# Cross-attention with a dense mixture of experts on one core: four slots of expert activations, one of down weights, and down rows spread over every expert step

## The reference

```python
q = layernorm(x) @ Wq + bq;  k = ctx @ Wk + bk;  v = ctx @ Wv + bv
x = x + softmax(q @ k.T / sqrt(256)) @ v          # for each of 16 sequences
h = layernorm(x)
router = softmax(h @ w_router); gate = softmax((h @ w_gating) / 0.1)
for e in range(8):                                # F = 1024
    expert[e] = (silu(h @ w_gate[e]) * (h @ w_up[e])) @ w_down[e]
cw = router * gate;  cw = cw / (sum(cw) + 1e-9)
out = x + sum_e expert[e] * cw[:, e]              # every expert sees every token
```

## Time and profile before

| | |
|---|---|
| profiled execution | 1101.56 us, of which the span of the core is 1099.8 us |
| PE busy | 1021.7 us (93%), 6160 matmuls |
| DVE busy | 789.0 us (72%) |
| POOL busy | 643.7 us (59%) |
| ACT busy | 499.1 us (45%) |
| mean granted TensorE clock | 0.969 of full |
| DMA | 40.61 MB, mean 37 GB/s |

### The profile page before, as it was taken

The page is one execution under the profiler, slowest core; times in us unless marked ns, Lnnn a source line. Parts: engine busy times, 40 slices in busy tenths (PEclk is TensorE's granted clock), DMA queues, the critical chain, the costliest instruction groups (busy, mean ns, idle before and its releaser), DMA issues.

```text
span 1099.8 us, 16297 instructions
## 1 busy us (share of the span) xinstructions
PE 1021.7 (93%) x6160; PEld 941.5 (86%) x6160; DVE 789.0 (72%) x1361; ACT 499.1 (45%) x874; POOL 643.7 (59%) x532
## 2 busy tenths in 40 slices
PE   6877787999999999999999999999999999999998
PEld 5877776988888888888888889988888888888888
DVE  4876737777777777777777777777777777777775
ACT  3676545444444443444444434444444444444432
POOL 3456526666656566666665656565666666565632
PEclk7898887999999999999999999999999999999999
DMA  6121104000101010101010101010100101010001
GB/s 164 69 91 54 37 12 150 26 33 21 39 20 40 20 39 20 40 11 40 8 40 20 39 20 39 20 39 20 38 21 20 39 21 39 20 39 1 1 1 67
DMA packets 37462, 40.61 MB, mean 37 GB/s; under 512 B 2760, under 2 KB 35384, under 8 KB 37384
## 3 DMA queue, kind: packets, MB, share of 16 engines
q1 hardware_dynamic: 37384, 39.58, 11.5%
HBM read 35.90 MB, written 3.67 MB: 36 GB/s over the span
## 4 chain that ended last, share of the span: by engine, by line
PE 53%; DVE 24%; POOL 10%; issue 4%; ACT 4%; DMA 4%; DVEq 0%; SPq 0%; POOLq 0%; ACTq 0%
PE ps L248 51%; POOL arena L411 7%; DVE xsacc L867 3%; DMA shared<-in_ctx 3%; DVE shared L856 2%; DVE shared L811 2%; DVE shared L833 2%; DVE shared L827 2%; DVE shared L813 2%; DVE shared L819 2%; ACT arena L594 2%; DVE shared L831 2%; DVE shared L846 2%; DVE shared L851 2%; DVE shared L837 1%
## 5 line engine op out<-in xcount | busy, mean ns | idle before, releaser
L411 POOL TENSOR_TENSOR arena<-shared,arena 128x448 fp32r<-128x448 f32 x256 | 311.7, 1233 | 309.1 <-ACT arena L594 306.2
L248 PE MATMUL ps<-arena 128*128 128x256 f32 (+4 forms) x3120 | 425.3, 289 | 7.8 <-DVE arena L252 5.5
L248 PEld LDWEIGHTS ps<-arena 128*128 128x128 f32 (+2 forms) x3120 | 414.4, 194 | 15.0 <-DVE arena L252 4.5
L248 PE MATMUL ps<-xc_hi,w_hi 128*128 128x448 f32 x896 | 342.0, 382 | 38.0 <-DVE shared L807 17.1
L248 PE MATMUL ps<-xc_lo,w_hi 128*128 128x448 f32 x896 | 329.8, 368 | 0.0
L248 PE MATMUL ps<-xc_hi,w_lo 128*128 128x448 f32 x896 | 329.8, 368 | 0.0
L248 PEld LDWEIGHTS ps<-xc_hi,w_hi 128*128 128x128 f32 x896 | 170.9, 191 | 80.3 <-DVE shared L807 28.2
L587 ACT ACTIVATE shared<-shared 128x448 f32<-128x448 f32 x192 | 109.6, 580 | 203.3 <-DVE shared L817 119.1
L248 PEld LDWEIGHTS ps<-xc_hi,w_lo 128*128 128x128 f32 x896 | 170.3, 190 | 14.4
L248 PEld LDWEIGHTS ps<-xc_lo,w_hi 128*128 128x128 f32 x896 | 171.2, 191 | 9.0
L594 ACT CAST arena<-shared 128x448 fp32r<-128x448 f32 x256 | 141.1, 567 | 75.6 <-DVE shared L851 55.4
(11 more groups left out here) (123 smaller groups left out, 930.0 us busy)
## 6 DMA issues: line engine op xcount, KB each, us to landing
early<-in_L_ffn_w_down SPq DMA_DIRECT2D x16, 512.0 KB, 3.9
shared<-in_ctx SPq DMA_DIRECT2D x8, 750.0 KB
w_raw<-in_L_ffn_w_gate SPq DMA_DIRECT2D x17, 256.0 KB, 2.8
w_raw<-in_L_ffn_w_up SPq DMA_DIRECT2D x17, 256.0 KB, 3.1
early<-in_L_ffn_w_gate SPq DMA_DIRECT2D x15, 256.0 KB, 2.7
early<-in_L_ffn_w_up SPq DMA_DIRECT2D x15, 256.0 KB, 3.1
x_dram<-xsacc SPq DMA_DIRECT2D x8, 224.0 KB, 5.6
xsacc<-x_dram SPq DMA_DIRECT2D x1, 1792.0 KB, 10.7
```

The costliest lines, as they stand in the source:

```text
L248: ins = nc.tensor.matmul(dst, w, m, start=first and i == 0, stop=last and i == len(passes) - 1, skip_group_check=onto)
L411: nc.gpsimd.tensor_tensor(h[:, 1, j, at:at + TC], tile, h[:, 0, j, at:at + TC].bitcast(fp32), ALU.subtract).then_inc(hid_lo_done, 1)
```

## The change

1. **Slots.** `HSLOTS` is 4, `wd` has one slot. ACT rounds the down weights of a half only when PE has finished all row tiles of the half before (`row_ready`), now in the third quad of the half itself, and POOL's low part follows. SP issues the load of the next down weights behind the two weight sets.
2. **Down rows.** In PE's list the row tiles of group g are 0 and 1 at the end of the even quad, 2, 3 and 4 in the odd quad, 5 and 6 in the next even quad; DVE's `add_rows` move accordingly.
3. **Temporaries.** `u21` and `u12` have two tiles each, by the parity of the quad; `up_u2` and ACT's `up_first` wait for the low parts of quad n-2.
4. **Combine weights** are computed on DVE at the ends of quads 1 and 2 and awaited in quad 3.
5. **Attention.** Contexts are loaded by halves (one sequence each) with a semaphore for each, and earlier at the start. `norm_terms` on POOL has two operations instead of four; DVE makes the other two (`tensor_scalar`). `maxima` and the exponentials are done for each sequence apart. POOL's preparing work is moved behind later parts (`low_set(0)` behind `add_bv(4)`, `low_set(1)` to the end of pair 7), `high_comb` and `high_set(1)` on ACT and the sums of `xf` on DVE to other pairs.

In the fence are the parts that the prediction speaks of; renamings are left out.

```diff
-    HSLOTS = 3
+    HSLOTS = 4
...
+        u21 = [up_t[:, 0, :], sb("u21_odd", [P, TC])[:, :]]
+        u12 = [up_t[:, 1, :], xsacc[:, TILES * D:TILES * D + TC]]
         g21, g12, g22, g11 = [gate_t[:, i, :] for i in range(4)]
-        u21, u12, u22 = [up_t[:, i, :] for i in range(3)]
+        u22 = up_t[:, 2, :]
...
-        HS, WD = 2 * 2 * TH, 2 * FT * D
-        hs = [arena[:, a:a + HS].rearrange("p (l j t) -> p l j t", l=2, j=2) for a in (0, 2 * HS + WD, HS)]
-        wd = [arena[:, a:a + WD].rearrange("p (l t d) -> p l t d", l=2, t=FT) for a in (3 * HS + WD, 2 * HS)]
+        hs = [arena[:, a:a + HS].rearrange("p (l j t) -> p l j t", l=2, j=2) for a in (0, 2 * HS + WD, HS, 3 * HS + WD)]
+        wd = arena[:, 2 * HS:2 * HS + WD].rearrange("p (l t d) -> p l t d", l=2, t=FT)
...
+            def load_ctx_half(p, b):
+                sp.dma_start(ctx_raw[:, p % 2, b], ctx_v[p][:, b]).then_inc(ctx_in[p % 2][b], DMA)
+            load_ctx_half(0, 0)
...
-            sp.dma_start(ctx_raw[:, 0], ctx_v[0]).then_inc(ctx_in, DMA)
+            load_ctx_half(0, 1)
             sp.dma_start(xs[:, 2:4, :], x_v[:, 2:4, :]).then_inc(x_parts[1], DMA)
+            for b in range(2):
+                load_ctx_half(1, b)
+            sp.dma_start(wv_raw, wv.rearrange("(k p) n -> p k n", p=P)).then_inc(wv_in, DMA)
...
             def load_ctx(p):
-                sp.wait_ge(ctx_in, DMA * p)
-                at_least(sp, ct_ready, 2 * (p - 1))
-                at_least(sp, cn_lo_done, 2 * (p - 1))
-                sp.dma_start(ctx_raw[:, p % 2], ctx_v[p]).then_inc(ctx_in, DMA)
+                for b in range(2):
+                    sp.wait_ge(ct_ready, 2 * (p - 2) + b + 1)
+                    sp.wait_ge(cn_lo_done, 2 * (p - 2) + b + 1)
+                    load_ctx_half(p, b)
...
             for hn in range(1, SETS):
                 if hn + 1 < SETS:
-                    load_down(hn + 1)
                     load_set(2 * hn + 2)
                     load_set(2 * hn + 3)
+                    load_down(hn + 1)
...
-            def norm_terms(mv, var, root, shift, bias, n, steps, done):
-                nc.gpsimd.tensor_tensor(var, mv[:, :, 1], eps_c[:, 0:n], ALU.add).then_inc(norm_step, 1)
-                pool.wait_ge(norm_step, steps + 1)
+            def norm_terms(var, root, shift, bias, n, step, done):
                 nc.gpsimd.tensor_tensor(root, var, power_c[:, 0:n], ALU.pow).then_inc(norm_step, 1)
-                pool.wait_ge(norm_step, steps + 2)
-                nc.gpsimd.tensor_tensor(shift, mv[:, :, 0], root, ALU.mult).then_inc(norm_step, 1)
-                pool.wait_ge(norm_step, steps + 3)
-                nc.gpsimd.tensor_tensor(bias, zero_c[:, 0:n], shift, ALU.subtract).then_inc(done, 1)
...
+                pool.wait_ge(norm_step, step)
+                nc.gpsimd.tensor_tensor(bias, shift, root, ALU.mult).then_inc(done, 1)
...
             def high_down(hn):
                 sc.wait_ge(wd_in, DMA * (hn + 1))
-                if hn > 1:
-                    sc.wait_ge(row_ready, RT * CP * (hn - 1))
-                nc.scalar.copy(wd[hn % 2][:, 0, :, :], wd_raw).then_inc(wd_hi_done, 1)
+                at_least(sc, row_ready, RT * CP * hn)
+                nc.scalar.copy(wd[:, 0, :, :], wd_raw).then_inc(wd_hi_done, 1)
...
             def up_first(n):
-                at_least(sc, hid_lo_done, 4 * (n - 1) + HID21)
-                first_product(n, up_prod, u21, u_a, up_p1)
+                at_least(sc, hid_lo_done, 4 * (n - 2) + HID21)
...
-                if p == 6:
-                    high_comb(0, COMB_SPLITS[0:3])
...
-                if p == 4:
+                if p == 5:
+                    high_comb(0, COMB_SPLITS[0:3])
+                if p == 6:
                     high_set(1)
...
-                    high_hidden(n - 1, HID21, u21, 0, TC)
-                    high_hidden(n - 1, HID12, u12, 1, 0)
+                    high_hidden(n - 1, HID21, u21[(n - 1) % 2], 0, TC)
                     up_first(n)
...
+                if turn == 2 and hn > 0:
+                    high_down(hn)
...
-            def maxima(p):
-                for b in range(2):
-                    ve.wait_ge(scores_ready, 2 * p + b + 1)
-                    ins = nc.vector.tensor_reduce(top[:, b:b + 1], ps_s[b][:, 0:TK], AX.X, ALU.max)
-                ins.then_inc(top_done, 1)
+            def maxima(p, b):
+                ve.wait_ge(scores_ready, 2 * p + b + 1)
+                one = slice(b, b + 1)
+                nc.vector.tensor_reduce(top[:, one], ps_s[b][:, 0:TK], AX.X, ALU.max).then_inc(top_done, 1)
                 ve.wait_ge(q_bk_done, p + 1)
-                ve.wait_ge(top_done, p + 1)
-                nc.vector.scalar_tensor_tensor(top_all[:], q_bk[:], c0[:, 0:1], top[:], ALU.add, ALU.add).then_inc(top_all_done, 1)
-                ve.wait_ge(top_all_done, p + 1)
-                nc.vector.scalar_tensor_tensor(neg_top[:], q_bk[:], c0[:, 0:1], top_all[:], ALU.add, ALU.subtract).then_inc(neg_top_done, 1)
+                ve.wait_ge(top_done, 2 * p + b + 1)
+                nc.vector.tensor_scalar(top_all[:, one], q_bk[:, one], c0[:, 0:1], top[:, one], ALU.add, ALU.add).then_inc(top_all_done, 1)
+                ve.wait_ge(top_all_done, 2 * p + b + 1)
+                nc.vector.tensor_scalar(neg_top[:, one], q_bk[:, one], c0[:, 0:1], top_all[:, one], ALU.add, ALU.subtract).then_inc(neg_top_done, 1)
...
+                nc.vector.tensor_scalar(var2[:], mv2[:, :, 1], EPS, None, ALU.add)
+                nc.vector.tensor_scalar(shift2[:], mv2[:, :, 0], -1.0, None, ALU.mult).then_inc(stats2_done, 1)
...
-                nc.vector.tensor_tensor(u12, u_x, u21, ALU.add).then_inc(up_sum, 1)
+                if n == 1:
+                    ve.wait_ge(x1_stored, DMA * PAIRS)
+                    ve.wait_ge(xn2_done, PAIRS)
+                at_least(ve, hid_lo_done, 4 * (n - 1))
+                nc.vector.tensor_tensor(u12[n % 2], u_x, u21[n % 2], ALU.add).then_inc(up_sum, 1)
...
+                at_least(ve, hid_lo_done, 4 * (n - 1) + HID22)
+                nc.vector.tensor_tensor(u22, u_x, u21[n % 2], ALU.add).then_inc(up_sum, 1)
...
                 if inside(p + 1):
                     ct_low(p + 1, 1)
                     q_low(p + 1)
                 if inside(p - 1):
                     residual1(p - 1)
                     stats2(p - 1)
-                if p == 1:
-                    stats1(14, B)
+                if p == 5:
+                    sums_1_3(0)
             for p in range(PAIRS):
...
             def quad(n):
-                g = n // FPAIRS - 1
-                odd = n % FPAIRS
+                g, odd = n // FPAIRS - 1, n % FPAIRS
                 if n > 1:
                     gate_u2(n)
+                    if n == 3:
+                        ve.wait_ge(cw_ready, 1)
+                        ve.wait_ge(acc_in, DMA)
                     if odd:
-                        add_rows(g, 2, ps_r[2])
-                        add_rows(g, 3, ps_r[3])
+                        add_rows(g, 0, ps_r[0])
+                        add_rows(g, 1, ps_r[1])
+                    elif g > 0:
+                        add_rows(g - 1, 4, ps_r[4])
+                        add_rows(g - 1, 5, ps_r[5])
                     up_u2(n)
                 gate_u3_c22(n)
                 if n > 1 and odd:
-                    add_rows(g, 4, ps_r[4])
-                    add_rows(g, 5, ps_r[5])
+                    add_rows(g, 2, ps_r[2])
+                    add_rows(g, 3, ps_r[3])
                 up_u3_c22(n)
-                if n == 1:
-                    combine_weights()
-                if n == 2:
-                    ve.wait_ge(cw_ready, 1)
-                    ve.wait_ge(acc_in, DMA)
-                if n > 1 and odd:
-                    add_rows(g, 6, ps_r[6])
+                if g > 0 and not odd:
+                    add_rows(g - 1, 6, ps_r[6])
                 gate_c21_c12(n)
                 hidden11(n)
-                if n > 1 and not odd:
-                    add_rows(g, 0, ps_r[0])
-                    add_rows(g, 1, ps_r[1])
                 hidden22(n)
                 up_c21(n)
...
                 g = n // FPAIRS - 1
                 gate_1_6_5(n)
                 if n % FPAIRS:
+                    down(g, 2)
+                elif g > 0:
+                    down(g - 1, 5)
+                up_1_6_5(n)
+                if n % FPAIRS == 0 and g > 0:
+                    down(g - 1, 6)
+                gate_2_7(n)
+                if n % FPAIRS:
+                    down(g, 3)
+                up_2_7(n)
+                gate_4_3(n)
+                if n % FPAIRS:
                     down(g, 4)
-                up_1_6_5(n)
-                if n % FPAIRS:
-                    down(g, 5)
-                gate_2_7(n)
-                up_2_7(n)
-                down(g, 6 if n % FPAIRS else 0)
-                gate_4_3(n)
-                if n % FPAIRS == 0:
-                    down(g, 1)
                 up_4_3(n)
```

(6 more changed lines are left out.)

200 lines of the change are left out of this document (101 added, 99 removed).

## The result

The changed kernel takes 1036.95 us, median of 4 runs (1035.68 to 1038.66), beside 1100.45 us for the kernel before on the same chip (4 runs, 1096.51 to 1100.64): a ratio of 0.943, 95% interval 0.941 to 0.946. The profiled execution took 1038.66 us with a span of 1036.9, that is 62.9 us less in the span than before. 1031 was predicted, with a range of 1015 to 1060.

The account below looks back on a forecast made before the run. PE was taken as the bound, busy 806.78 of 835.65 us in quads 4 to 61, waiting only for gate_u2 and up_u2. Terms summed to -70.0 from 1101.56, giving 1031.6, predicted as 1031 us, range 1015 to 1060.

Parts of the forecast that it names:

- The expert loop: Quads 4 to 62: gate_u2 and up_u2 no longer late, a pair of quads from 28.82 to 27.17 us, -49.5 us.
- the chain of four: Even quads: DVE's L811, L813, L831, L833 must follow PE without a tile; 0.1 us a pair kept for it.
- A: Rival: DVE's chain in the even quad becomes the bound, 29 stalls of some 0.9 us, 1057 us; chance 0.13.
- C: Rival: row tile 0 waits for the single down-weight slot's refill in each half, slower, 1136 us at W = 7; chance 0.04.
- The zero for the single slot: Third quad of each half: PE's wait on wd_done at row tile 0 costs 0, between 0 and +51 us.
- D: Rival: the expert loop's stall stays at 28.82 us a pair and only the start changes, 1080 us; chance 0.02.
- Attention: Start to quad 2: start -3, pairs 3 to 6 -17.0, pair 7 +2.5 us.
- The sign that was named for it: Pairs 3 to 5 at 11 to 13 us, no wait for contexts, granted clock there at 1.0.
- The pairs 3, 4, 5 have pair 2's conditions ... I take 12.0: Attention: contexts land before they are wanted, so these pairs take 12.0 us each; pairs 3 to 6 together -17.0.
- Pair 6 ... 17.5: Attention: pair 6 keeps route and gets high_comb ahead of its own ACT work, taking 17.5 us.
- Start ... -3: Start of attention: first context half loaded ahead of biases, context 1 not waiting for context 0; -3, between -6 and +2.
- Rival B: Attention gains nothing but its start: extra small DVE operations can meet POOL's L367 and hold exponentials; 1048 us, chance 0.13.

Follow-up runs that it names:

- loop-alone run: The kernel before with only the change's expert loop (parts 1 to 4), its attention untouched: 1043.68 us, ratio 0.950 to the kernel before.

## Why the prediction was right, and where a term was not

**The expert loop** was right by its mechanism and nearly by its size: -53.9 from quad 2 on where -52.5 was predicted. The wait for `gate_u2` goes because the tile ahead of up 1 and the one ahead of gate 2 give DVE cover; the layout said 2.2 us to spare, the trace says 3.35, since DVE's tail ends 1.15 earlier as well. The 0.1 us a pair kept for the chain of four was not lost: 27.09 instead of 27.17. What the layout did not say is that the rows alone do it; the prediction named parts 2 and 3 together, and the temporaries turned out to be a second cure of part of the same illness.

The stretch from quad 2 on came out close because small misses cancel. The 30 pairs of quads from quad 4 on brought 51.9 (30 x 1.73) where 49.5 was predicted. Quads 2 and 3 brought 5.1 (28.10 instead of 33.20) and the tail cost 3.1 (17.90 instead of 14.78 behind quad 63), together -2.0 where -3.0 was predicted: in quad 2 a wait of 1.86 and some half clock are left, and the gap for POOL's low part ahead of the last rows, which was to close, is 1.38 instead of 1.08. Two sums in the prediction are off by little: the tail's 4.2 and 1.4 make 5.6 us and not 5.2 (measured: 4.42), and the bounds of its own terms make a worst case of 1057 and not 1050, still inside the range.

One reading stopped a step short. `hidden12` is named as what makes `gate_u2` late, but not why it takes 1.58 us. It reads two tensors in SBUF, and POOL's low parts (L411) run beside it. Where POOL is idle, one quad on, the same operation takes 0.61. Lines of POOL and DVE before the change:

```profile
509.76 5.24 POOL L411 TENSOR_TENSOR arena<-shared,arena 128x448 fp32r<-128x448 f32 x4 [3.46 <-ACT arena L594]
...
523.54 1.16 POOL L411 TENSOR_TENSOR arena<-shared,arena 128x448 fp32r<-128x448 f32 x1 [1.16 <-ACT arena L594]
...
525.11 0.61 DVE L861 TENSOR_TENSOR shared<-shared 128x448 f32<-128x448 f32 x1
```

From 206 to 1050 us it takes 1.57 to 1.58 in 29 quads, those ahead of the 29 waits for `gate_u2`, and 0.61 in the 30 others. So 0.97 us of lateness stood in front of a wait of 0.57, from the kind of collision that the next paragraphs find in attention. Whether the wait would have gone without it was not tried; in the changed kernel `hidden12` is still held (1.57), and the tiles hide it.

**Rivals.** A did not come: 0.35 us of spare was enough 29 times. C did not come in the changed kernel, 1.07 us of spare, but it did at once where row tile 0 stood in its old place, 15 times 1.58 us. The zero for the single slot was right because of part 2 of the change, and the margin is three quarters of the 1.43 that the window of 4.87 against 3.44 suggested. D is refuted by the waits.

**Attention** is the step that was mis-sized. -17.5 from the start to quad 2 was predicted, -9.0 came (about -6 as its own share, by the loop-alone run). The sign that was named for it came in part: no wait for contexts in pairs 3 to 5, but 17.02 us in pair 3, and a granted clock of 0.93, 0.95 and 1.00.

- "The pairs 3, 4, 5 have pair 2's conditions ... I take 12.0" held for pairs 4 and 5 (11.26 and 10.96), and failed for pair 3, with 17.02. `low_set(0)` was moved off norm2's way and onto that of `times_bk`. With one wait more for POOL, pair 3 takes 11.83. That is 5 of the 8.5 missing us.
- "Pair 6 ... 17.5" was 20.61. The rows show the mix waiting for ACT's roundings, but moving these brought nothing in the end. It may be the chain of sums, roundings and low parts of `xf` that sets pair 6; which link is worth what stays open. One link is held by POOL too: a sum of `xf` (L797) with two inputs in SBUF takes 2.55 us from 112.40, beside L368, where its like (L792) takes 0.62 at 102.52.
- "Start ... -3" was +0.8. Pair 1 starts at 29.70 instead of 35.73, and then takes 19.86 instead of 13.78: the statistics of sequences 4 to 7, which now come in pair 0, stand ahead of `ct_low` and `q_low` on DVE and release norm1 of pair 2 too late. Moved again, they brought the start of pair 3 forward by 0.7.

**Rival B** deserves the closest look. "Each extra small DVE operation can meet a running L367 and hold the exponentials": I counted operations and overlooked that the same lines of the diff change their form. As TENSOR_SCALAR, with one tensor and two columns of scalars, they are not held (0.27 us beside POOL's L368); as SCALAR_TENSOR_TENSOR they cost 10 us, and the attention changes would have been worth less than nothing (1046.92 beside 1043.68 for the loop alone). So B's price was right, for a form of the operations that the change does not have. The page that the prediction drew on (the Trainium skill, SBUF — State Buffer, Who interferes with whom) limits its rule in just this way: a DVE instruction contends if it has two SBUF inputs while GpSimd reads SBUF, or runs in a mode that takes both ports. By that the trace agrees, in both directions, if columns of scalars are not counted as inputs; `times_bk`, with two tensors from SBUF, is held like the rest, and the subtractions of L253 that read one operand from PSUM are not (0.94 us at 66.83, beside L368). Where page and trace differ is on how long: the same page of the Trainium skill (Summary: rules for kernel authors) has the second one wait until the first finishes, but `neg_top` waited through three POOL instructions in a row (5.10 us) and `top_all` through four (9.19 us).

## What to carry to other kernels

When work on an engine comes in bursts, lay out one round with all engines and put independent work where the others need time; that was worth 50 us here, and it made the second tiles for `u21` and `u12` all but unnecessary. When GpSimd work is moved, list what DVE runs at its new time with two operands in SBUF: a collision of 4 us cost 5 of the 17.5 that attention was to gain, and a wait added on the engine that was not late took it back. Check a small operation's form, not its size.

## What was not expected of the hardware

- An operation of 112 x 1 numbers stood for up to 9.19 us behind GpSimd, and three GpSimd instructions that began after it went ahead of it. Changing its form was worth 10 us of 1047.
- A short stall can have a price behind it, and the same stall can have none. In quad 2 of the changed kernel PE waited 1.86 us, the granted clock is 0.54 from 184.70 to 187.00, and the next nine matmuls are 0.37 us and more apart instead of 0.203: 1.6 us more. In the loop-alone run it waited 1.83 us at the same place, and the clock stayed at 1.00. What makes the difference no run shows. These are the first and the last of the nine:

```profile
184.75 0.65 PE L249 MATMUL ps<-xc_hi,w_hi 128*128 128x448 f32 x1 [1.86 <-DVE shared L809]
...
187.81 0.58 PE L249 MATMUL ps<-xc_hi,w_lo 128*128 128x448 f32 x1
```

- The stalls of 0.57 and 0.43 in each even quad of before did not have that price: the granted clock was 1.00 over the whole loop. A pair of quads lost 1.73 us to them (28.82 to 27.09), of which the waits in the rows are 1.0; the rest shows as wider spacing of the matmuls around them, for example 0.31 us instead of 0.20 from 513.71 to 514.02.
